# Node rows made block by block behind the added expert rows, old rows loaded by groups in the last stage

## The reference

```python
x = x + _L0_gnn_ref(_layernorm(x), edge_index, edge_weight, ...)   # 5 rounds of message passing with a GRU
x = x + _L0_ffn_ref(_layernorm(x)[None], ...)[0]                   # top-1 of 8 experts
x = x + _L1_gnn_ref(_layernorm(x), L1_gnn_W, L1_gnn_a, src, dst)   # graph attention, 8 heads
x = x + _L1_ffn_ref(_layernorm(x)[None], ...)[0]                   # top-2 of 16 experts, then gamma, beta

# _L0_ffn_ref:  H = gelu(xf @ W1 + b1); probs = softmax(H @ Wg + bg); the best expert e alone:
#               out = probs[:, e] * (H @ Wd[e] + bd[e])
# _L1_gnn_ref:  h = x @ W; per edge and head:
#               lin = hs.a1 + hd.a2 + (hd - hs).a3 + |hd - hs|.a4 + (hs * hd).a5
# _L1_ffn_ref:  y = x + moe;  out = (y - mu) / sqrt(var + EPS) * gamma + beta
```

## Time and profile before

| what | us |
|---|---|
| median of 3 runs | 6366.73 |
| lowest, highest of them | 6354.01, 6389.2 |
| the profiled execution, its own time | 6352.31 |
| its span, first to last instruction | 6350.7 |
| PE busy | 4473.9 (70%) |
| DVE busy | 2786.1 (44%) |
| POOL busy | 2421.8 (38%) |
| ACT busy | 1761.4 (28%) |
| mean granted TensorE clock | 0.866 |

### The profile page before, as it was taken

The page is one execution under the profiler, slowest core; times in us unless marked ns, Lnnn a source line. Parts: engine busy times, 40 slices in busy tenths (PEclk is TensorE's granted clock), DMA queues, the critical chain, the costliest instruction groups (busy, mean ns, idle before and its releaser), DMA issues. The chain is left out here.

```text
span 6350.7 us, 62482 instructions
## 1 busy us (share of the span) xinstructions
PE 4473.9 (70%) x17114; PEld 2665.0 (42%) x17114; DVE 2786.1 (44%) x6353; ACT 1761.4 (28%) x4039; POOL 2421.8 (38%) x2837
## 2 busy tenths in 40 slices
PE   1111323348899999999998887577777776997794
PEld 0010101124544544544544365455555555664462
DVE  7994000023354344353223124544444447777435
ACT  4331000000100000000000312345455546997121
POOL 3787777720000000000001013666666664886024
PEclk9999655579899999999999887788888887998697
DMA  8700122137332222221322233566666663776323
GB/s 353 291 1 25 58 75 75 58 118 254 130 123 85 87 98 85 97 91 69 114 99 86 94 117 99 162 197 200 200 201 198 199 202 122 242 243 215 114 63 107
DMA packets 381089, 865.15 MB, mean 136 GB/s; under 512 B 87346, under 2 KB 187732, under 8 KB 353369
## 3 DMA queue, kind: packets, MB, share of 16 engines
q1 hardware_dynamic: 250281, 686.15, 30.8%
q0 software_dynamic: 76816, 147.75, 9.0%
q10 hardware_dynamic: 53664, 27.26, 1.5%
HBM read 576.84 MB, written 284.11 MB: 136 GB/s over the span
## 5 line engine op out<-in xcount | busy, mean ns | idle before, releaser
L1110 PE MATMUL PS<-mem 128*128 128x512 f32 (+1 forms) x3500 | 1465.2, 575 | 387.9 <-issue 255.9
L1110 PEld LDWEIGHTS PS<-mem 128*128 128x128 f32 x3500 | 655.3, 201 | 1173.0 <-issue 1035.0
L1990 POOL DMA_INDIRECT mem<-gat_rows,mem x832 | 814.2, 979 | 463.8 <-issue 441.6
L1291 POOL TENSOR_TENSOR mem<-mem 128x256 f32<-128x256 f32 x25 | 20.2, 842 | 2137.4 <-DMA mem<-x 2137.4
L581 POOL DMA_INDIRECT adjacency_more<-mem x526 | 544.6, 1035 | 171.0 <-issue 171.0
L2098 DVE TENSOR_TENSOR mem<-mem,PS 128x512 f32<-128x512 f32 x416 | 285.6, 687 | 645.4 <-ACT mem L2071 484.3
L1176 ACT ACTIVATE mem<-PS 128x512 f32<-128x512 f32 (+1 forms) x35 | 19.1, 545 | 1912.9 <-PE PS L1110 1355.2
L2033 PE MATMUL PS<-mem 128*128 128x256 bf16 x2496 | 428.5, 305 | 169.3 <-issue 143.3
L2401 PE MATMUL PS<-mem 128*128 128x264 f32 x1660 | 461.3, 407 | 7.9 <-DVE mem L2352 3.6
L1220 DVE COPY mem<-PS 128x512 f32<-128x512 f32 (+1 forms) x35 | 21.9, 625 | 951.7 <-PE PS L1110 649.3
L262 PE MATMUL PS<-mem 106*128 106x106 f32 (+4 forms) x446 | 102.0, 373 | 477.4 <-DVE mem L393 303.4
(11 more groups left out here) (405 smaller groups left out, 7070.9 us busy)
## 6 DMA issues: line engine op xcount, KB each, us to landing
mem<-adjacency SPq DMA_DIRECT2D x150, 1280.0 KB
gathered_rows<-mem SPq DMA_DIRECT2D x416, 264.0 KB
mem<-gathered_rows SPq DMA_DIRECT2D x208, 528.0 KB, 4.5
adjacency<-mem SPq DMA_DIRECT2D x56, 800.0 KB, 20.8
adjacency_more<-mem SPq DMA_DIRECT2D x56, 800.0 KB
mem<-adjacency_more SPq DMA_DIRECT2D x30, 1280.0 KB
adjacency<-mem SPq DMA_DIRECT2D x30, 1280.0 KB
mem<-edge_slots ACTq DMA_DIRECT2D x26, 1024.0 KB
```

The lines of the kernel that those rows point to most:

```text
L1110: ins = t.matmul(PS[:, f, 0:n], lhsT=h[:, b, f * 128:(f + 1) * 128], rhs=m.pan[i % NPAN][:, j, 0:n], start=(b == 0), stop=(b == NB - 1))
L1990: g.indirect_dma_start(m.Dg[i % RING][:, k, j, :], None, HD[:, :], bass.IndirectOffsetOnAxis(ap=L.idxD[:, c:c + 1], axis=0)).then_inc(s[f" ...
```

## The change

**Hidden** loses `gt`, `gT` and the load of `bd`.

**Experts.** `bd` is now spread over all partitions (1 MB) and DVE adds the chosen expert's bias when it takes a tile out of PSUM; the expert's number is read into registers. The bias phase at the end is gone. The join behind the stage is gone too: its tail and the nodes stage are one. The gathers back have 5 semaphores and each block its own buffer, in the memory of `AT`. The weights of the nodes stage are loaded as the experts start, and the coefficients are made within DVE's loop over the tiles, after tile 4.

**Nodes.** DVE's loop does, in iteration i: the added rows and statistics of block i; every five blocks the reciprocal and shift of the group before; the low part of block i-17; reduce and logits of block i-10; the rest of block i-14. ACT's iteration i: normalizes block i (all 25 now on ACT), copies the turned block i-1, copies row i-3 and squares it out of PSUM, high part of i-7, middle part of i-10, and each fifth a square root. There are 6 PSUM banks for rows and 4 buffers for squares and rests. POOL runs its gathers 12 blocks ahead of its one multiply. The 16 loads into `PEN` are issued once all of X is new and block 15 is stored, since `PEN` and `AT` hold other data until then.

**Finish.** Old rows come in five loads of 640 KB, `beta` as one row; PE puts old rows plus `beta` in PSUM with two matmuls; DVE centres before it waits for the deviation, and groups end at blocks 5, 10, 15, 20, 24 and 25.

```diff
 def experts_vector(...):
-            v.tensor_copy(m.og[j % 2], PS[:, 4 + j % 2, 0:256]).then_inc(s["og"].sem, 1)
-    for b in range(NB):
-        n = rows_of(b)
-        v.wait_ge(*s["bd_ps"](b + 1))
-        v.tensor_tensor(h.X[:, b, :], h.X[:, b, :], PS[:, 7, 0:256], ALU.add).then_inc(s["bd"].sem, 1)
...
+            if j % 8 == 0:
+                v.reg_load(regs, m.eo[0:1, j:j + 8])
+            e = v.snap(regs[j % 8], min_val=0, max_val=7 * 8)
+            v.tensor_tensor(m.og[j % 2], PS[:, 4 + j % 2, 0:256], nd.bd[:, bass.ds(e * 32, 256)],
+                            ALU.add).then_inc(s["og"].sem, 1)
+        if i == 4:
+            nodes_coefficients(v, nd, ns, st)
+NU = 4
+NBANK = 6
+ROWS_AT, REST_AT, LOW_AT = 10, 14, 17
+GATHERS_AHEAD = 12
 def nodes_sync(...):
     for b in range(NB):
         q.wait_ge(*s["logits"](2 * b + 2))
         q.dma_start(HD[b * 128:(b + 1) * 128, :], m.HB[:, b, 8:272]).then_inc(s["stored"].sem, 16)
+        if b == NB - ROWS_AT:
+            q.wait_ge(*s["x_new"](NB))
+            for r in range(16):
+                row = SEGD[r * LROW:(r + 1) * LROW + 2, 0]
+                q.dma_start(m.PEN[8 * r:8 * r + 8, :], row.unsqueeze(0).partition_broadcast(8)).then_inc(s["pen"].sem, 16)
 def nodes_scalar(...):
-    ln_scalar(c, m.ln, s, m.Y, m.X, epsc)
+    def deviations(k):
+        w = slice(5 * k, 5 * k + 5)
+        c.wait_ge(*s["mv"](5 * k + 5))
+        c.activation(m.ln.sd[:, w], m.ln.mv[:, w, 1], ACT.Sqrt, bias=epsc).then_inc(s["sd"].sem, 1)
+    deviations(0)
+    for i in range(NB + 10):
         if i < NB:
+            c.wait_ge(*s["nb"](i // 5 + 1))
+            c.activation(m.Y[:, i, :], m.X[:, i, :], ACT.Identity, bias=m.ln.nb[:, i:i + 1],
+                         scale=m.ln.sd[:, i:i + 1]).then_inc(s["y"].sem, 1)
...
+        if 3 <= i <= NB + 2:
+            b = i - 3
             c.wait_ge(*s["rows_ps"](b + 1))
+            c.activation(m.HB[:, b, 8:264], PS[:, b % NBANK, 0:256], ACT.Copy).then_inc(s["rows"].sem, 1)
+            if b >= NU:
+                c.wait_ge(*s["hq"](b - NU + 1))
+            c.activation(m.u1[b % NU], PS[:, b % NBANK, 0:256], ACT.Square).then_inc(s["square"].sem, 1)
+        if 7 <= i <= NB + 6:
+            b = i - 7
...
+        if i % 5 == 4 and i + 1 < NB:
+            deviations(i // 5 + 1)
+def nodes_gpsimd(g, x, m, s, es, YS0):
...
+    for b in range(NB + GATHERS_AHEAD):
+        if b < NB:
+            if b >= NYG:
+                g.wait_ge(*s["x_new"](b - NYG + 1))
+            g.indirect_dma_start(m.yg[b][0:n], None, YS0[:, :], ...)
+        if b >= GATHERS_AHEAD:
+            k = b - GATHERS_AHEAD
+            g.wait_ge(*s["square"](k + 1))
+            g.tensor_tensor(u, u, m.a5h, ALU.mult).then_inc(s["fifth"].sem, 1)
+def nodes_vector(v, h, m, s, es, PS):
+    for i in range(NB + LOW_AT):
+        if i < NB:
+            v.wait_ge(*es[f"yg{i % NYG}"](16 * (i // NYG + 1)))
+            v.scalar_tensor_tensor(x, m.yg[i][0:n], h.pmx[0:n, i:i + 1], x, ALU.mult, ALU.add).then_inc(s["x_new"].sem, 1)
+            ... bn_stats, bn_aggr of block i
+        if i % 5 == 0 and 5 <= i <= NB:
+            ... wait sd(i // 5), reciprocal, nb
+        if i >= LOW_AT: ...            # low part of i - 17, waits for mid
+        if ROWS_AT <= i < NB + ROWS_AT: ...  # reduce and logits of i - 10, waits for fifth
+        if REST_AT <= i < NB + REST_AT: ...  # rest of i - 14, waits for high
+ENDS = (5, 10, 15, 20, 24, 25)
+def finish_tensor(t, f, cn, s, PS):
+    for b in range(NB):
+        if b % GRP == 0:
+            t.wait_ge(*s[f"xl{b // GRP}"](16))
+        if b >= 8:
+            t.wait_ge(*s["rows"](b - 7))
+        t.matmul(PS[:, b % 8, 0:256], lhsT=cn.ident, rhs=f.X[:, b, :], start=True, stop=False)
+        t.matmul(PS[:, b % 8, 0:256], lhsT=cn.ones[0:1, :], rhs=f.bt, start=False, stop=True).then_inc(s["kept"].sem, 1)
 def finish_vector(...):
-        if b % GRP == GRP - 1:
-            for c in range(b0, b + 1):
-                v.tensor_tensor(f.X[:, c, :], f.X[:, c, :], f.bt, ALU.add).then_inc(s["xb"].sem, 1)
+        if b + 1 in ENDS:
...
-                v.scalar_tensor_tensor(m.Y[:, c, :], m.Y[:, c, :], f.sd[:, c:c + 1], f.X[:, c, :],
+                v.scalar_tensor_tensor(m.Y[:, c, :], m.Y[:, c, :], f.sd[:, c:c + 1], PS[:, c % 8, 0:256],
```

More of the change, by code:

```diff
@@ L1713, in experts_scalar, with experts_vector @@
                      ACT.Copy).then_inc(s["cp_a"].sem, 1)
[L1714 to L1721, removed]
+def experts_vector(v, m, h, nd, cn, s, ns, st, PS, regs):
     route_vector(v, m.r, cn, s, st, PS, h.OH)
@@ L1782, in nodes_memory, with nodes_weights @@
     m.Y = ar.mk(NB, D)
+    m.yT = [ar.mk(2, 128) for _ in range(2)]
+    m.u1 = [ar.mk(256) for _ in range(NU)]
+    m.hq = ar.mk(8)
+    m.R = [ar.mk(NROW) for _ in range(NU)]
+    m.ln = ln_memory(ar)
+    top, ar.top = ar.top, early
     m.Wa = ar.mk(2, 272)
-    m.av5 = ar.mk(5, 256)
+    m.a5h = ar.mk(256)
+    m.a45 = ar.mk(4)
     m.msk = ar.mk(8)
[L1786 to L1801, removed]
+    m.A = ar.mk(248)
+    early_end, ar.top = ar.top, top
+    return m, early_end
+NU = 4
+NBANK = 6
+ROWS_AT, REST_AT, LOW_AT = 10, 14, 17
+GATHERS_AHEAD = 12
+NODES = {"w": 80, "bias": 16, "pen": 256, "x_new": NB, "stats": NB, "mv": NB, "sd": 5, "rsd": 5, "nb": 5, "y": NB, "coef": 1, "half": 1,
+         "zero": 1, "weights": 1, "slots": 16, "yt_ps": NB, "yt": NB, "rows_ps": NB, "rows": NB, "square": NB, "fifth": NB,
+         "hq": NB, "logits": 2 * NB, "high": NB, "rest": NB, "mid": NB, "low": NB, "stored": 16 * NB}
+def nodes_weights(q, a, m, s):
+    q.dma_start(m.bd, spread(a["bd"].rearrange("e d -> (e d)"))).then_inc(s["bias"].sem, 16)
     q.dma_start(m.Wa[:, :, 0:256], a["Wgat"].rearrange("(k p) n -> p k n", p=128)).then_inc(s["w"].sem, 16)
@@ L1806, in nodes_sync @@
     q.dma_start(m.msk, a["c_mask"]).then_inc(s["w"].sem, 16)
[L1807 to L1809 removed]
+def nodes_sync(q, m, L, s, HD, SEGD, SLD):
+    q.dma_start(SLD.rearrange("(r n) o -> r (n o)", r=104), L.slT[0:104]).then_inc(s["slots"].sem, 16)
     for b in range(NB):
@@ new lines, in rows @@
+    def rows(lo, hi):
+        q.wait_ge(*s["rows"](hi))
+        q.dma_start(out[lo * 128:hi * 128, :].rearrange("(b p) d -> p b d", p=128),
+                    m.Y[:, lo:hi, :]).then_inc(s["out"].sem, 16)
+    q.dma_start(f.gm, spread(a["gamma"])).then_inc(s["w"].sem, 16)
+    q.dma_start(f.bt, a["beta"].unsqueeze(0)).then_inc(s["w"].sem, 16)
+    kept(0)
+    kept(1)
+    for k in range(2, GRP):
+        kept(k)
+        rows(GRP * (k - 2), GRP * (k - 1))
+    for k in range(3, len(ENDS) - 1):
+        rows(ENDS[k - 1], ENDS[k])
@@ L2819, in finish_scalar, with finish_vector @@
 def finish_scalar(c, f, s, epsc):
-    for k in range(GRP):
-        w = slice(GRP * k, GRP * k + GRP)
-        c.wait_ge(*s["mv"](GRP * k + GRP))
-        c.activation(f.sd[:, w], f.mv[:, w, 1], ACT.Sqrt, bias=epsc).then_inc(s["sd"].sem, 1)
-def finish_vector(v, m, f, s, st):
+    lo = 0
+    for hi in ENDS:
+        c.wait_ge(*s["mv"](hi))
+        c.activation(f.sd[:, lo:hi], f.mv[:, lo:hi, 1], ACT.Sqrt, bias=epsc).then_inc(s["sd"].sem, 1)
+        lo = hi
+def finish_vector(v, m, f, s, PS):
+    lo, groups = 0, 0
     for b in range(NB):
```

224 lines of the change are left out of this document (106 added, 118 removed).

## The result

The changed kernel takes 6340.4 us (median of 20 runs, 6327.4 to 6376.6), the kernel before beside it 6368.3 us (20 runs, 6350.0 to 6402.3). The ratio is 0.9962, 95% interval [0.9949, 0.9975]: 24 us less, with 16 to 32 left open (the two medians lie 28 us apart). 6334 had been forecast, 33 us less.

A forecast was written before the change was run, and what follows sets the result against it. No engine bounds the whole; each stage by its own chain, the nodes stage next by its `PEN` loads. Nodes 23.5, last stage 9 and hidden 0.4 make 33 us: 6366.7 - 33 = 6334, range 6306 to 6350.

The forecast's parts named there:

- Three phases over each other, the experts' stage unchanged: Phases of 50, 21 and 67 us before the logits overlap; the experts' bias and coefficients cost at most about 1 us.
- T, the issue of the loads: Nodes stage: SP issues the 16 loads into `PEN` at 3930, bounds 3926 to 3940.
- The loads bind: Join before the logits: `PEN` loads end the stage, first gather at 3986, gain 23.5 us instead of 54.
- Rival 1: Nodes stage: `PEN` loads run faster and don't bind; arithmetic ends at 3955, whole gain 63 us, time 6304; chance 10%.
- 16 x 208 KB = 3.4 MB at some 70 GB/s is 48 us: Nodes stage: how long the `PEN` loads take, from their issue at 3930 to their end at 3978.
- 25 us after T: Nodes stage: after the loads' issue 17 iterations without an added row remain, 10 x 1.73 and 7 shorter; ends at 3955.
- Rival 2: Nodes stage: ACT's square roots bring extra table loads, 10.3 us; loads issued 5 to 12 us later, time 6343; chance 19%.
- Rival 3: Nodes stage: DVE's and ACT's groups take turns, 25 us a group; 4 us slower, time 6371; chance 5%.
- Eight engines for the loads: `PEN` loads: 8 partitions make 8 DMA engines by the skill's rule, in agreement with a busy share of 0.50.
- The tail: End of the last stage: 1.3 us after the statistics instead of 5.7, gain 4.4; last stores gain another 1.1.
- The last stage's other 3.5 us: Last stage, POOL's gathers: one stall behind DVE's group work goes, 1.5 us, and long gathers shorten, 2 us.
- The sum: Whole kernel: 23.5 + 9 + 0.4 = 33 us less, median 6334, 0.52% less; chance 0.52 of over 0.5% faster.

The follow-up runs named there:

- e2: Changed kernel with the `PEN` loads as 8 transfers of 16 strided partitions instead of 16 of 8; ratio 0.9914 to the kernel before.
- e1: The changed kernel again, for a second trace and a base; ratio 0.9981 to the kernel before.
- e3: Changed kernel with the `PEN` loads issued behind the last block's store instead of block 15's; ratio 0.9989 to the kernel before.
- e4: Changed kernel with the last stage of the kernel before; ratio 0.9961 to the kernel before.
- e9: The kernel before run again unchanged, for a second trace; one run, logits' gathers 1289.5 us from first to last.
- e5: Kernel before with only the changed last stage, on the other kind of chip; ratio 0.9989, last stage 80.2 us.

## Why the prediction was right, and where its sizes were off

- **Three phases over each other, the experts' stage unchanged: right.** From the first gather of the experts' stage to the first gather of expert rows it takes 152.7 us, and 150.8 to 152.8 in the other kernels with the new nodes' stage; before, 152.0 and 151.5. So the bias and the coefficients cost less than 1 us, if anything.
- **T, the issue of the loads: right.** 58.6 us after the first gather of expert rows; the prediction's 3930.3 is 57.5 after that gather before, at 3872.8. DVE stood for the second square root at iteration 10 for 4.3 us, and 1 us once more.
- **The loads bind: right, and shown** (e2 takes 40 us off the stretch by changing them alone). Rival 1, that they don't, is out: 43 idle us.
- **The term "16 x 208 KB = 3.4 MB at some 70 GB/s is 48 us": mis-sized, and the largest error.** It was read off bandwidth while they ran before. They last 55.8 us in the changed kernel, and 56.6 to 57.6 in e1, e3 and e4, at 3.4 to 3.6 us a packet; where the kernel before issues them it is 46.0 us (2.85) in one trace and 50.5 (3.17) in the other. So 61.4 us from T to the gather instead of 55.7. With 1.1 us of T this makes the gain 16.7 us by the two traces instead of 23.5.
- **Why they are slower with less beside them, the packets' times suggest.** The 128 packets run eight at a time. How far apart eight successive ones start, against how long one takes (medians by turns of eight, behind the first turn):
```
trace                         eight starts within   one packet
late loads (e3)               0.4 us                3.59 us
changed again (e1), at first  0.2 us                3.64 us
  then                        1.2 us                3.52 us
changed, at first             0.3 us                3.63 us
  then                        1.4 us                3.39 us
before again (e9), at first   1.9 us                3.18 us
  then                        2.3 us                2.92 us
before, at first              1.8 us                2.92 us
  then                        2.2 us                2.57 us
last stage alone (e5)         2.2 us                2.52 us
```
  The more nearly the eight go in step, the slower each is, also within one trace at the moment one of them falls out of step; e3 has nothing beside the loads and 3.59 us. Where the kernel before issues them, behind other loads of the queue, the first eight start within 0.7 to 1.8 us of each other (before, e9, e5), in the changed kernels within 0.1. Going in step alone doesn't slow them: in e2, with 16 source rows, eight successive ones start within 0.5 to 0.8 us and one takes 2.05. Eight engines that read one row of memory at the same moment would fit all of this; no run changes that alone, so it isn't shown. What the term did was to carry a rate over from loads that had started apart to loads that start together.
- **The arithmetic, "25 us after T": it ends 18.1 us after it** (3931.3). Nine iterations with logits were left, not ten, and they took 14 us (1.3 us each where nothing is waited for, not 1.73), the seven shorter ones 4.2, not 7.7; a rest there takes DVE 0.42 us, not the 0.61 of the earlier trace rows. The arithmetic didn't bind, so this moved nothing.
- **Rival 2, ACT slow: wrong.** The single table load above shows that `Square` brought no switch after a square root. The Trainium skill (ScalarE: Activation LUTs, What ACT_TABLE_LOAD costs) puts a switch at about 2.66 us, by which eight would have been 21 us, an estimate; the trace has none in the stage. Rival 3, groups that take turns: wrong, DVE is busy 46.5 of 59 us.
- **Eight engines for the loads:** the trace's share of 0.46 to 0.56 while they run with next to nothing beside them (0.51 in e3), and 0.94 with 16 partitions a transfer, agree with the rule of the Trainium skill (DMA: Bandwidth & Descriptors, why a DMA increments its semaphore by 16). The number of engines accounts for the factor 2; the other factor of 1.66 is a packet's own time.
- **The tail: right.** From the end of the last aggregation to the last row 1.2 us (forecast 1.3), 4.5 us less than before (4.4 forecast). From there to the end of the span it is 2.0 us less (1.1 forecast).
- **The last stage's other 3.5 us: wrong.** "POOL's stall goes, and half of the long gathers": from the first gather to the last aggregation the changed kernel takes 80.0 us, the kernel before 78.2 and 78.7. The first added row does come early (5.5 us after the first gather, before 8.8 and 9.0), and POOL's stall behind the group comes back as 6.6 us when DVE's hand-overs are late. On the other kind of chip it is 74.7 (e5). So 5 us of gain instead of 9. What the old last stage takes on that kind of chip has no trace.
- **The sum.** 33 us were worked out; by the parts it is 21 to 22, from 6366.7 some 6345. The measured 6340.4 is between. So the mechanism was right and two terms were too large, the loads by 5.7 us and the last stage by 4; that the median came within 7 us of 6334 owes something to luck, as the same kernel's second series lay 12 us nearer to the kernel before. Of the chances, 0.52 had gone to more than 0.5% faster and 0.44 to within 0.5%: the less likely of the two came, since with 33 us the sum stood just past that bound.

## What to carry to other kernels

When phases are laid over each other, look for the transfer whose issue moves later with them: its length, not the engines' sums, ends the new stage. Look at its shape first: eight partitions a transfer gave 61 GB/s, sixteen with rows that differ 204. A rate read from a trace holds for the company and the start that the transfers had there. Compare stages by landmarks, and take a second trace of the kernel before, before explaining a difference of 1.5% in a stage that nobody touched.

## What was not expected of the hardware

- Chips of two kinds: 6350 to 6402 us against 5862 to 5914 for the kernel before, mean granted clock 0.864 to 0.868 against 0.891 to 0.897. Over 200 us of it are in the logits' stage (1289 against 1067), whose bound changes from late hand-overs between engines to POOL's gathers; the clock of this stage is 0.83 (e9) and 0.89 (e5).
- A packet of 26.6 KB took 2.5 to 3.6 us where eight partitions are filled from one row of memory, the longer the more the eight went in step, and 2.05 us where 16 are filled from 16 rows.
- Right behind these 16 loads SyncE's issue of a 132 KB store took 10 to 14 us three times, where it is 0.3 to 0.5 us otherwise (changed and e1). In the kernel before, whose stores follow the loads by 18 us, and in e2, whose loads are fast, none did.
- On the first kind of chip, two dependent instructions of DVE stood up to 1.3 us apart for over 10 us, in a stretch that six traces have at the same place.
